# The last of four expert layers computed over routed rows in blocks of 128 instead of over all tokens, in a one-core Flamingo-style kernel

## What is computed

```python
def _L3_ffn_ref(x, w_router, w1, b1, w2, b2):          # x: layer norm of the residual, 1024 x 128
    logits = xf @ w_router                             # 8 experts
    probs = jax.nn.softmax(logits, axis=-1)
    topk_w, topk_idx = jax.lax.top_k(probs, 2)
    mask = jax.nn.one_hot(topk_idx, 8)
    weights = jnp.sum(topk_w[..., None] * mask, axis=1)
    h = jax.nn.gelu(jnp.einsum('te,ieh->tih', xf, w1) + b1)     # 128 -> 512 per expert
    out = jnp.einsum('tih,ihe->tie', h, w2) + b2                # 512 -> 128
    return jnp.sum(out * weights[..., None], axis=1)
x = x + jnp.tanh(g_ffn[3]) * _L3_ffn_ref(_layernorm(x), ...)
```

## Time and profile before

| what | value |
|---|---|
| runs shown | 943.76, 948.68, 1962.34 us; median 948.68 |
| the profiled execution's own time | 943.48 us |
| its span | 941.7 us, so 1.8 us lie around it |
| TensorE busy | 766.1 us, 81% of the span |
| VectorE, ScalarE, POOL busy | 462.1, 395.4, 137.1 us |
| mean granted TensorE clock | 0.902 |
| last expert layer (first logits to end of the span) | 815.3 to 941.7 us |

### The profile page before, as it was taken

The page is one execution under the profiler, slowest core; times in us unless marked ns, Lnnn a source line. Parts: engine busy times, 40 slices in busy tenths (PEclk is TensorE's granted clock), DMA queues, the critical chain, the costliest instruction groups (busy, mean ns, idle before and its releaser), DMA issues.

```text
span 941.7 us, 12265 instructions
## 1 busy us (share of the span) xinstructions
PE 766.1 (81%) x4480; PEld 507.0 (54%) x4480; DVE 462.1 (49%) x1144; ACT 395.4 (42%) x942; POOL 137.1 (15%) x205
## 2 busy tenths in 40 slices
PE   2042589856779999799999768999999678899997
PEld 2030246635542333267677446767777458677775
DVE  6977923277776775262113589341121448432112
ACT  4010114245414777653344367543332646643332
POOL 1012100023130000010301134302300213200000
PEclk9565779969886999999999879999999899999999
DMA  9100015000493000300011100000102000000100
GB/s 356 57 1 0 0 45 179 6 1 2 128 223 51 2 3 1 135 1 1 31 38 46 67 1 1 1 1 23 45 23 78 12 1 1 1 1 1 45 12 12
DMA packets 16802, 38.48 MB, mean 41 GB/s; under 512 B 1174, under 2 KB 10707, under 8 KB 16483
## 3 DMA queue, kind: packets, MB, share of 16 engines
q1 hardware_dynamic: 16742, 37.69, 12.7%
HBM read 32.35 MB, written 5.24 MB: 40 GB/s over the span
## 4 chain that ended last, share of the span: by engine, by line
PE 66%; DVE 24%; ACT 5%; issue 4%; DMA 1%; POOL 0%; SPq 0%; DVEq 0%; ACTq 0%; POOLq 0%
PE PS L1543 18%; PE PS L1527 18%; PE PS L1659 4%; PE PS L1354 3%; PE PS L1621 3%; DVE NTOP L1030 3%; PE PS L1649 3%; DVE MX L1162 2%; DVE BIG L1031 2%; PE PS L1310 2%; PE PS L1260 1%; DVE XH L787 1%; PE PS L1364 1%; PE PS L1502 1%; PE PS L1340 1%
## 5 line engine op out<-in xcount | busy, mean ns | idle before, releaser
L1543 PEld LDWEIGHTS PS<-RINGW,BIG 128*128 128x128 f32 x1536 | 178.8, 192 | 22.0 <-issue 22.0
L1543 PE MATMUL PS<-RINGW,BIG 128*128 128x128 f32 x1536 | 179.3, 275 | 0.3 <-PE PS L1543 0.3
L1087 DVE SCALAR_TENSOR_TENSOR ACC<-PS,GC,ACC 128x128 f32<-128x128 f32 x192 | 54.1, 344 | 252.1 <-PE PS L1543 222.9
L1527 PE MATMUL PS<-HTR,RINGW 128*128 128x512 f32 x384 | 175.5, 602 | 2.6 <-PE PS L1543 1.5
L689 ACT ACTIVATE BIG<-PS,Wt 128x512 f32<-128x512 f32 x128 | 86.5, 685 | 89.0 <-PE PS L1527 88.6
L1527 PEld LDWEIGHTS PS<-HTR,RINGW 128*128 128x128 f32 x384 | 70.2, 192 | 76.1 <-issue 75.9
L1162 DVE TENSOR_REDUCE MX<-PS 128x2 f32<-128x1024 f32 x64 | 78.5, 1226 | 25.5 <-PE PS L1621 23.7
L1354 PE MATMUL PS<-BIG 128*128 128x128 f32 x400 | 56.6, 293 | 8.7 <-DVE TMP L1212 3.1
L477 POOL TENSOR_TENSOR BIG<-BIG,REC 128x616 f32<-128x616 f32 x40 | 48.6, 1215 | 94.6 <-DVE REC L1040 94.6
L1354 PEld LDWEIGHTS PS<-BIG 128*128 128x128 f32 x400 | 51.2, 203 | 17.6 <-issue 10.6
L689 ACT ACTIVATE BIG<-PS 128x512 f32<-128x512 f32 x64 | 37.9, 598 | 38.3 <-PE PS L1527 37.8
(11 more groups left out here) (277 smaller groups left out, 1068.0 us busy)
## 6 DMA issues: line engine op xcount, KB each, us to landing
RINGW<-up SPq DMA_DIRECT2D x40, 512.0 KB, 3.8
scratch<-RINGW SPq DMA_DIRECT2D x12, 384.0 KB, 4.6
Wt<-wpack SPq DMA_DIRECT2D x1, 2992.5 KB
BIG<-scratch SPq DMA_DIRECT2D x2, 1024.0 KB
Ct<-cpack SPq DMA_DIRECT2D x1, 1568.0 KB
BIG<-scratch SPq DMA_DIRECT2D x2, 768.0 KB
Rt<-rpack SPq DMA_DIRECT2D x1, 717.5 KB
X<-x SPq DMA_DIRECT2D x1, 512.0 KB, 3.4
```

Source lines behind the costliest of these rows:

```text
L1087: ins = v.scalar_tensor_tensor(out=ACC[:, t, :], in0=PS[:, 4 + g % 2, j * D:(j + 1) * D], scalar=GC[:, t, e:e + 1], in1=ACC[:, t, :], op0= ...
L1527: mm(PS[:, ch, :], RINGW[:, slot, ch * P:(ch + 1) * P], HTR[:, cols(b)], start=True, stop=True)\
L1543: ins = mm(PS[:, 4 + g % 2, j * D:(j + 1) * D], HB[g % 2][:, ch, j * P:(j + 1) * P], RINGW[:, slot, F + ch * D:F + (ch + 1) * D], start=(c ...
```

## The change

1. `moe(3)` is replaced by `blocks`. Each half of 512 tokens has 1024 (token, expert) rows. They are put into 15 blocks of 128 rows, each block with one expert: blocks 0 to 7 belong to experts 0 to 7, and blocks 8 to 14 go to whichever experts have more than 128 rows (7 such blocks always suffice). The number of blocks is fixed at 30; unused rows hold other finite numbers.
2. Routing per half. `half_logits` (4 mm) and `half_exp`; `route_probs` and `route_picks` on VectorE give the two experts; `half_ranks` (14 small bf16 mm with a triangle of ones) counts for each row how many came before it; `route_slots` turns ranks into row numbers (`slot_int`) and names the experts of blocks 8 to 14 (`expert_int`). For half 0 this stands in steps 16 to 20 of `cross_tiles(3)`; for half 1 the first part stands ahead of block 0 and the ranks after block 2.
3. Scatter: POOL writes rows of `XH` to a DRAM buffer `rows[b]` with 8 indirect DMAs per half (`dispatch`, 128 rows of 512 bytes each). SP waits for all 8 and reads the buffer back in three DMAs (`load_rows`).
4. Blocks: TensorE turns 4 blocks of rows at a time (`rows_turn`), ScalarE copies them (`rows_out`); per block 4 mm of 128x128 (`first`), four gelus of 128x128, 4 mm of 128x128 (`second`), a VectorE copy to one of four buffers `YS`, and a 64 KB store to the place of the block in `rows[b]` by SP. `first(n + 1)` is issued ahead of `second(n)`.
5. Expert weights are loaded once per block: 24 loads beyond the first six, each issued by SP when block n-6 is done; for blocks 8 to 14 of a half SP first reads the expert's number from SBUF.
6. Return: once all 15 blocks of a half are stored POOL fetches them with 8 indirect DMAs; VectorE multiplies by the two gates and adds (`combine`), then `finish`. Half 0 is combined after the copy of block 23, half 1 at the end.
7. `b1` travels with the weights (1028 columns instead of 1024), for all expert loads of levels 1 to 3. At the start SP fills the two row buffers (1.2 MB each) from DRAM once the sixteen experts of level 0 have been issued.
8. The semaphores of the three cross attentions become one set that counts on from level to level (`sem("x_s_exp")`, `UNITS0[k] + s - 1` in place of `sem(f"s{k}_exp")`, `s - 1`). The same waits stand at the same places.

```diff
+BLOCKS = 15
+ROWS = BLOCKS * P + N
 @sync
-            load_experts(E0 + RING, E0 + 3 * E)
+            load_experts(E0 + RING, E0 + 2 * E + RING)
+            def load_block(n):
+                b, i = n // BLOCKS, n % BLOCKS
+                if i < E:
+                    src = up[2 * E + i]
+                else:
+                    if i == E:
+                        sp.wait_ge(sem("experts_known"), b + 1)
+                    src = up[sp.value_load(ROUTE[b].expert_int[0:1, i - E:i - E + 1], min_val=0, max_val=E - 1) + 2 * E]
+                sp.wait_ge(sem("block_out"), n - RING + 1)
+                ...
+            def load_rows(b):
+                sp.wait_ge(sem(f"dispatched{b}"), 16 * 2 * HT)
+                ...
+            load_rows(0)
+            for n in range(2 * BLOCKS):
+                if n + RING < 2 * BLOCKS:
+                    load_block(n + RING)
+                if n == 9:
+                    load_rows(1)
+                sp.wait_ge(sem("block_copied"), n + 1)
+                b, i = n // BLOCKS, n % BLOCKS
+                sp.dma_start(rows[b][i * P:(i + 1) * P, :], YS[n % 4]).then_inc(sem(f"block_stored{n % 4}"), 16)
 @gpsimd
+            def dispatch(b, t):
+                for i in range(2):
+                    at = bass.IndirectOffsetOnAxis(ap=ROUTE[b].slot_int[:, i, t:t + 1], axis=0)
+                    nc.gpsimd.indirect_dma_start(rows[b], at, XH[:, HT * b + t, :], None).then_inc(sem(f"dispatched{b}"), 16)
+            pool.wait_ge(sem("slots_known"), 1)
+            for t in range(2):
+                dispatch(0, t)
             ln(1)
+            for t in range(2, HT):
+                dispatch(0, t)
+            pool.wait_ge(sem("slots_known"), 2)
+            for t in range(HT):
+                dispatch(1, t)
+            for b in range(B):
+                for m in range(4):
+                    last = max(n for n in range(BLOCKS * (b + 1)) if n % 4 == m)
+                    pool.wait_ge(sem(f"block_stored{m}"), 16 * (last // 4 + 1))
+                for t in range(HT):
+                    for i in range(2):
+                        at = bass.IndirectOffsetOnAxis(ap=ROUTE[b].slot_int[:, i, t:t + 1], axis=0)
+                        nc.gpsimd.indirect_dma_start(YG[b][:, t, i, :], None, rows[b], at).then_inc(sem(f"returned{b}"), 16)
 @vector
+            def blocks(finish):
+                route_probs(1, logits_of(1))
+                route_picks(1)
+                for n in range(2 * BLOCKS):
+                    dve.wait_ge(sem("block_out"), n + 1)
+                    if n >= 4:
+                        dve.wait_ge(sem(f"block_stored{n % 4}"), 16 * (n // 4))
+                    v.tensor_copy(YS[n % 4], PS[:, 3 + n % 2, 0:D]).then_inc(sem("block_copied"), 1)
+                    if n == RANK_AT:
+                        route_slots(1)
+                    if n == BLOCKS + 8:
+                        combine(0)
+                        finish(0)
+                combine(1)
+                finish(1)
-            moe(3, 1, [finish])
-            finish(1)
+            blocks(finish)
 @tensor
+                    if k == 3 and s == ROUTE_AT:
+                        half_logits(0, tm + 1, w("L3f_router"))
+                    if k == 3 and s == ROUTE_AT + 3:
+                        half_ranks(0)
+            def blocks(m, norms):
+                ...
+                turn(m, 1, XH, "xh_ready", norms)
+                pe.wait_ge(sem("slots_known"), 1)
+                half_logits(1, m, w("L3f_router"))
+                rows_turn(0)
+                first(0)
+                rows_turn(1)
+                for n in range(2 * BLOCKS):
+                    if n + 1 < 2 * BLOCKS:
+                        first(n + 1)
+                    second(n)
+                    ...
-            moe(3, w("L3f_router"), E, 1, 18, None, None)
+            blocks(12, 18)
```

345 lines of the change are left out of this document (279 added, 66 removed).

## The result

The changed kernel takes 956.4 us (median of four runs, 954.93 to 959.57); the kernel before took 943.76, 945.27 and 948.68 us beside it, and once 1962.34, which is left out of the comparison. The ratio is 1.0115, 95% interval [1.0066, 1.0165]: slower beyond its uncertainty, by less than the 2% that the chances were set by. Forecast were 942.0 us; the execution profiled took 954.93, 953.1 of it span. So the time is 13 us above the forecast, and the gain in TensorE's work is real but eaten up.

The account below looks back on a forecast made before the run. TensorE was taken to bound the kernel. From a span of 941.7 us, TensorE's stretch -52.4, front +34.5 and tail +16.1 gave span 940, with 1.8 us around it 942; range 922 to 968.

Parts of the forecast that it names:

- The front: Routing, scatter and reading back of half 0 before the blocks: first second product at 849.8 us, +34.5 on the span.
- p: POOL's time for one indirect DMA, taken as 1.3 us; 16p on the path, each 0.1 us being 1.6 us.
- (B): Rival: cheap indirect DMAs, p = 0.5, without bubbles and DMA stalls: 924 us; chance 0.19.
- (A): Rival: dear indirect DMAs, p = 2.5, with half 1's rows and half 0's return late: 968 us; chance 0.17.
- the tail: Last product to end: copy, store, eight gathers, weighted sums, residual and last store, 20.6 us where 4.5 stood.
- The blocks themselves: TensorE's stretch over the 30 blocks: 63.5 us of work plus 6 on top, 69.5 us for 121.9 before.
- bubbles: TensorE's waits in the blocks for gelus and ScalarE's row copies: 3 us, bounds 0 to 8.
- the 2 us for DMA: Stalls in the blocks, DMA and TensorE being level at 40 us with five blocks of ring: 2 us, bounds 0 to 10.
- on top I take 6: Added to the blocks' 63.5 us: 3 us for bubbles, 1 for the clock, 2 for DMA.
- POOL's scatter of half 1 starts after block 2 ... fits: Beside the blocks: scatter from about 861, rows wanted about 883; 8p + 5 = 15 us fits up to p = 2.1.
- (C): Rival: DMA bounds half 0, 512-byte pieces at 0.6 us per 64 KB adding 11.5 us of work: 952 us; chance 0.12.
- (D): Rival: the first scatter is late, a start costing 1 us (943) or 6 us by the skill page (948); chance 0.04.

Follow-up runs that it names:

- gated_rows9: Changed kernel with half 1's scatter and half 0's gathers held in pairs for given blocks, half 1's rows read at block 9 before its load: 945.0 us, ratio 0.9968.
- no_loads: Changed kernel without the 24 weight loads of the later blocks and SP's reads of expert numbers: 944.1 us.
- no_stores: Changed kernel without the 30 stores of block results and the waits for them: 939.6 us.
- late_return: Changed kernel with half 0's gathers and combining moved after all 30 blocks: 950.9 us; blocks 69.9 us, 76.6 us when run again on another chip.
- first group: Four kernels built on the changed kernel (no_loads, no_stores, late_return, paced), run on one chip without the unchanged kernel: 944.1, 939.6, 950.9 and 967.9 us.
- no_scatter1: Changed kernel without the scatter of half 1, whose rows SP reads without waiting: span 946.2 us, blocks 77.3 us.
- no_loads_again: The no_loads kernel (changed kernel without the 24 weight loads) run a second time, in another group: span 953.2 us, blocks 81.4 us.
- half_rows: Changed kernel with half 1's scatter and half 0's gathers moving 64 rows per indirect DMA instead of 128: span 958.6 us, blocks 86.6 us.
- plain_scatter: Changed kernel with half 1's tokens written by eight plain POOL DMAs in token order, half 0's gathers still indirect: span 945.8 us, blocks 77.2 us.
- after_again: The changed kernel itself, profiled a second time and timed in three more rounds: ratio 1.0115 to the kernel before, blocks 83.7 us.
- paced: Changed kernel with POOL waiting for each indirect DMA to land in half 1's scatter and half 0's gathers: 967.9 us.

## Why the prediction was wrong

**Right.** The front to within 1 us in sum; p = 1.26 for 1.3, against rivals at 0.5 (B) and 2.5 (A), though the quarter added to POOL's 1.04 was a guess that happened to fit; the clock at 0.50 before the blocks; the tail, 19.4 for 20.6, where each of its terms is found in the timeline. The blocks themselves: 69.5 forecast; gated_rows9, which does the whole work, takes 69.5, and no_loads, no_stores and late_return on the first group's chip 67.3 to 69.9. That both figures are 69.5 is in part luck: in gated_rows9 TensorE is busy for 63.3 and idle for 6.3 of it; the waits for ScalarE are 5.3 us where 3 were put for bubbles, and the 2 us for DMA did not come. The bubbles are where they were put: TensorE waits 0.8 us for ScalarE wherever it also copies rows. The counting semaphores and the fill cost nothing that shows in this pair of executions: TensorE's transposes beside the cross attention's tile 6 stand at 808.64 us in the changed kernel's trace and at 808.70 in that of the kernel before, and half 0's row numbers come 2 us before the forecast.

**Wrong.** The step that failed is "on top I take 6" together with "POOL's scatter of half 1 starts after block 2 ... fits": it asked only whether POOL would be ready in time, and took a POOL that works beside the blocks for free. It was in time (half 1's rows and half 0's return were there when wanted), but while it issues eight indirect DMAs the hand-over from TensorE to the others stops. That is the missing term. The forecast put it at nothing; beside gated_rows9 the changed kernel's blocks are 84.95 - 69.54 = 15.4 us longer, 12.0 of them more idling of TensorE (18.2 against 6.3) and 3.4 more time in products (66.7 against 63.3), at the lower clock. The first standstill alone costs 6.4 to 6.7 (no_scatter1, late_return); the second alone 7.8 (no_scatter1's 77.3 beside gated_rows9's 69.5, on another chip). No rival had this mechanism. (C), DMA as the bound, gives nearly the time (952) and is refuted: no_loads_again has the standstill with a third of the traffic (6.66 MB instead of 19.31 from 815 to 955 us), half_rows with half the rows. (D) came out small: the first indirect DMA took 1.21 us instead of 0.96. By the Trainium skill's "GPSIMD Engine Reference" (Instruction dispatch) the first call of fresh code costs 6 us; here the rest of the front leaves no room for it.

**DMA stalls.** By the rule of the Trainium skill's "DMA: Bandwidth & Descriptors" (Why small descriptors are slow) that was weighed, the 2 us of DMA stalls would not come. In the changed kernel no wait of TensorE in the blocks ends with a load or with rows (its 13.3 us end with ScalarE's gelus but for 0.8), so in this point the rule's result was the better one; no run measures what a piece of 512 bytes costs.

**Misread, without effect.** The 2.6 us of the earlier trace rows is the shortest of all transfers to and from the ring; the expert loads alone land in 3.1 at the least, and 3.0 was taken for the rows. The logits of half 0 by half of 0.96 end at 809.9, not 810.4. The pieces behind the 198 GB/s of the earlier trace rows are not "1 KB and more": 3991 packets for 3.97 MB, 1 KB on the average.

**Open.** What inside the chip stops. Every engine that stood still waited for a signal of TensorE, whose products are recorded as done; but their ends are modelled, so the trace doesn't tell whether TensorE's work, its signals or the others' reading of them is late. Fetching of code is not enough by itself: no_scatter1 has a 16 KB code transfer at 864.3 us as the changed kernel has at 864.2, and no standstill there. Also open is why the first group's chip showed none in its five runs of eight, while all eighteen on the others did, fifteen in full and three in part: whether that is the chip or the hour isn't known. The first group alone would have led to the wrong cause.

## What to carry to other kernels

A run of indirect DMAs is not free because GpSimd is: look in the timeline whether the other engines wait for "remote" or "another core" beside it, and compare the end of a product with the start of its copy. Give them out in short runs tied to the progress of the loop (a count that is already there), not to their landings, and read what they wrote ahead of the bulk loads. And before an experiment that leaves a part out is believed, run the unchanged kernel on the same chip beside it: here three kernels "cured" a standstill that on their chip may not have occurred.

## What the runs showed of the hardware

- One indirect DMA costs GpSimd 0.94 to 1.00 us for 128 rows and 0.90 for 64 (half_rows), with 0.30 to the next; the first one of the program 1.21. A plain one costs 0.54 (4.33 for eight, plain_scatter).
- Eight in a row stop the hand-over from TensorE to ScalarE, VectorE and SyncE: in the changed kernel products that end 2.5 to 3.7 us after the first of them are copied 1.8 to 2.0 us late, the next ones 6.1 to 7.2, and ScalarE goes on 1.8 us after the last is issued. In the other runs it goes on 1.7 to 1.8 us after it in most, 0.2 at the earliest (after_again, gathers) and 2.3 at the latest (half_rows, with half the rows). Of 23 runs of eight beside products 15 show it in full, three in part, and five, all on one chip, not at all. Behind four in a row copies come up to 2.8 us late; at single pairs none does. The "Trainium skill" page "SBUF — State Buffer" (SBUF: two separate sides) says that a DMA can't be slowed by a compute operation nor the other way round. The trace agrees for what runs: TensorE's halves of a block take 0.89 us beside the DMAs as without them; it is the waiting between engines that grows.
- Beside the blocks an indirect DMA takes 2.2 to 5.5 us from issue to landing (paced), against some 2.5 at the end of the kernel, 945.05 to 947.61.
- After 6.35 us of an idle TensorE the granted clock is 0.50 from 872 to 876 us, 0.56 to 880 and 1.00 then; after 7.61 us it is 0.50 from 912 to 916, 0.87 to 920 and 1.00 then.
